# Attention values projected by channel and turned back, and slot inputs requested two slots ahead

## What is computed

```python
def attention(x, Wq, Wk, Wv, Wo):
    Q, K, V = x @ Wq, x @ Wk, x @ Wv
    logits = einsum('bqd,bkd->bqk', Q, K) * 128 ** -0.5
    attn = softmax(where(causal, -inf, logits))
    return einsum('bqk,bkd->bqd', attn, V) @ Wo

def ffn(x, ...):                          # cut to what matters
    xln = ln(x, ln1_w, ln1_b)
    x = x + sigmoid(xln @ Wr) * (xln @ Wv) @ Wo
    h = ln(x, ln2_w, ln2_b)
    winners = argmax(bids(h))             # one of 3 experts per row
    hr = square(relu(einsum('nc,ech->enh', h, K_rwkv)))      # two experts of 256 -> 1024 -> 256
    out_rwkv = einsum('enh,ehc->enc', hr, V_rwkv)
    out_trans = h @ W1 * sigmoid((xln @ Ws) @ W2) @ W3
    return x + chosen(out_rwkv, out_trans, winners) * scale

x = x + 0.5 * ffn(layernorm(x))
x = x + attention(layernorm(x))
x = x + 0.5 * ffn(layernorm(x))
```

## Time and profile before

| | us |
|---|---|
| median of 3 runs | 1089.14 (1087.94 to 1089.94) |
| the profiled execution | 1091.29 |
| span of its trace | 1089.5 |
| PE busy | 1000.6 (92%) |
| DVE, ACT, POOL busy | 691.2, 564.8, 496.5 |
| mean granted TensorE clock | 0.970 of full |

### The profile page before, as it was taken

How to read it: one execution, slowest core, us unless ns; L and a number is a source line. 1 busy time by engine, 2 the same in 40 slices (tenths; PEclk the granted TensorE clock), 3 DMA queues, 4 the chain that set the end, 5 groups by cost and what they waited for, 6 DMA issues and landing times.

```text
span 1089.5 us, 21438 instructions
## 1 busy us (share of the span) xinstructions
PE 1000.6 (92%) x7076; PEld 919.8 (84%) x7077; DVE 691.2 (63%) x1750; ACT 564.8 (52%) x1185; POOL 496.5 (46%) x541
## 2 busy tenths in 40 slices
PE   8999998959999999889988899899999699999997
PEld 7788886959999999778887788678888599999997
DVE  5688877836555554456765668578887764555553
ACT  5776655434454443245553555676664264444552
POOL 3254634456566556551221001135634576556665
PEclk8999998779999999999999999999999799999999
DMA  8621243122111111310222233402212222112211
GB/s 269 200 95 67 90 136 136 59 63 75 59 48 58 58 59 59 100 37 11 87 98 87 78 117 127 145 20 102 75 40 79 78 79 61 58 48 68 77 59 41
DMA packets 51845, 90.01 MB, mean 83 GB/s; under 512 B 5902, under 2 KB 44176, under 8 KB 50576
## 3 DMA queue, kind: packets, MB, share of 16 engines
q1 hardware_dynamic: 43120, 63.64, 18.7%
q0 software_dynamic: 8640, 25.24, 6.2%
HBM read 59.44 MB, written 47.85 MB: 98 GB/s over the span
## 4 chain that ended last, share of the span: by engine, by line
PE 66%; DVE 16%; DMA 6%; ACT 5%; issue 4%; POOL 3%; SPq 1%; DVEq 0%; POOLq 0%; ACTq 0%
PE banks4to L407 32%; PE bank L407 22%; PE banks4to L1694 3%; DMA slot_z<-routed_rows 2%; DVE out_rows L1053 2%; DVE pT_lo L1955 2%; PE bank L1227 2%; PE bank L503 1%; DVE gT_lo L955 1%; PE bank L1706 1%; DVE zT_lo L944 1%; DVE chunk_max L1945 1%; DMA attn_x<-x_after_ffn 1%; PE bank L371 1%; DMA routed_rows<-out_rows,row_index 1%
## 5 line engine op out<-in xcount | busy, mean ns | idle before, releaser
L1385 DVE TENSOR_TENSOR relu_squared<-relu 128x512 f32<-128x512 f32 x136 | 154.9, 1153 | 105.7 <-ACT relu L1336 55.3
L1451 POOL TENSOR_TENSOR hr_lo<-relu_squared,hr_hi 128x512 fp32r<-128x512 f32 x136 | 188.4, 1398 | 59.8 <-DVE relu_squared L1385 55.3
L1336 ACT ACTIVATE relu<-bank,slot_k_bias 128x256 f32<-128x256 f32 x204 | 84.8, 467 | 185.4 <-PE bank L407 168.0
L407 PE MATMUL banks4to<-v_hi,hr_hi 128*128 128x256 f32 x544 | 156.6, 288 | 3.7 <-DVE slot_out L1394 3.0
L407 PE MATMUL banks4to<-v_hi,hr_lo 128*128 128x256 f32 x544 | 153.3, 282 | 0.0
L407 PE MATMUL banks4to<-v_lo,hr_hi 128*128 128x256 f32 x544 | 153.3, 282 | 0.0
L407 PE MATMUL bank<-shT_hi,k_hi 128*128 128x256 f32 x408 | 116.9, 287 | 8.2 <-issue 5.4
L407 PE MATMUL bank<-shT_lo,k_hi 128*128 128x256 f32 x408 | 115.2, 282 | 0.0
L407 PE MATMUL bank<-shT_hi,k_lo 128*128 128x256 f32 x408 | 114.9, 282 | 0.0
L407 PEld LDWEIGHTS banks4to<-v_hi,hr_hi 128*128 128x128 f32 x544 | 103.5, 190 | 7.5 <-issue 7.0
L407 PEld LDWEIGHTS banks4to<-v_hi,hr_lo 128*128 128x128 f32 x544 | 103.5, 190 | 0.0
(11 more groups left out here) (279 smaller groups left out, 3031.7 us busy)
## 6 DMA issues: line engine op xcount, KB each, us to landing
routed_rows<-in_pad SPq DMA_DIRECT2D x34, 514.0 KB, 5.2
slot_row<-routed_rows SPq DMA_DIRECT2D x34, 258.0 KB
slot_z<-routed_rows SPq DMA_DIRECT2D x34, 256.0 KB
attn_x<-x_after_ffn SPq DMA_DIRECT2D x16, 256.0 KB, 2.9
attn_out<-x_after_ffn SPq DMA_DIRECT2D x16, 256.0 KB, 2.7
x_after_attention<-attn_out SPq DMA_DIRECT2D x16, 256.0 KB, 2.1
x_rows<-x_after_attention SPq DMA_DIRECT2D x8, 512.0 KB, 5.1
x_rows<-in_x SPq DMA_DIRECT2D x7, 512.0 KB, 4.0
```

The lines of the kernel that those rows point to most:

```text
L407: mm = pe.matmul(outv, w(pw), m(pm), start=(n_first and k == 0), stop=(n_last and k == 2))
L1336: last = act.activation(b.r[q % 2][:, (h % 2) * SLOT:(h % 2 + 1) * SLOT], b.bank(1 + q)[:, (h % 2) * SLOT:(h % 2 + 1) * SLOT], ACT.Relu, b ...
L1385: dve.tensor_tensor(b.sq[q % 2][:, :], b.r[q % 2][:, :], b.r[q % 2][:, :], ALU.mult).then_inc(f["sq"], 1)
L1451: pool.tensor_tensor(b.hr[p][1][:, 2 * q:2 * q + 2].rearrange("p h n -> p (h n)"), b.sq[q % 2][:, :], b.hr[p][0][:, 2 * q:2 * q + 2].rearr ...
```

## The change

Two edits that don't touch each other.

**Values.** `project_v` now holds the weights and streams the block's 256 rows, 2 x 3 = 6 matmuls of 256 columns. The result has channels on partitions. ACT copies it to a new tile `values_by_channel` (`v_turned`), PE turns its two halves back into columns 256 to 511 of the same bank (`turn_v`, 2 transposes), and only then come `v_hi` and `v_lo`. In the prologue the values of block k use bank k % 4 of banks 0 to 3, which takes V out of the ring there, and are turned after the next block's `project_qk`. In the steps they stay in the ring.

**Slots.** SP requests z two slots ahead: z of slots 0 to 3 before the wait for the late halves, then row(j), z(j+2).

In the diff the first piece is SP's, the pieces with `project_v` and `turn_v` are PE's, then one of ACT, and last two of DVE.

```diff
-    for j in range(2):
-        sp.dma_start(b.sz[j][:], rg[j][:, :, 0:C]).then_inc(f["s_in"][j], 16)
+    for j in range(4):
+        z_in(j, j % 2)
     sp.wait_ge(f["late"], 16 * GT * 2)
     for j in range(2):
-        sp.dma_start(b.srow[j][:, :, 0:ROW - C], rg[j][:, :, C:ROW]).then_inc(f["r_in"][j], 16)
-    with sp.Fori(0, (NSLOT - 3) // 2) as it:
+        row_in(j, j)
+    with sp.Fori(0, (NSLOT - 5) // 2) as it:
         for par in range(2):
-            slot_in(it * 2 + 2 + par, par)
-    slot_in(NSLOT - 1, 0)
+            row_in(it * 2 + 2 + par, par)
+            z_in(it * 2 + 4 + par, par)
...
     def project_v(k):
-        out = b.bank(k - QB + 4) if k in LATE_V else bank(("V", k))
+        out = b.bank(k % 4) if k < QB else bank(("V", k))
+        for c in range(CC):
+            mm = passes(pe, out[:, 0:SLOT], lambda p: b.Wvv[:, c, p * DK:(p + 1) * DK], lambda p: z_of(k)[p][:, c],
+                        c == 0, c == CC - 1)
+        mm.then_inc(a["V"], 1)
+
+    def turn_v(k):
+        pe.wait_ge(a["vt"], k + 1)
+        to = value_slot(k)
         for t in range(ST):
-            for c in range(CC):
-                mm = passes(pe, out[:, t * DK:(t + 1) * DK], lambda p: z_of(k)[p][:, c, t * P:(t + 1) * P],
-                            lambda p: b.Wvv[:, c, p * DK:(p + 1) * DK], c == 0, c == CC - 1)
-        mm.then_inc(a["V"], 1)
+            mm = pe.transpose(v_bank(b, k)[:, SLOT + t * DK:SLOT + (t + 1) * DK], b.vt[:, 2 * to + t], b.ident[:])
+        mm.then_inc(a["VN"], 1)
...
         project_qk(k)
+        if 0 <= k - 1 and k - 1 not in LATE_V:
+            turn_v(k - 1)
         if k not in LATE_V:
+            if k >= 4:
+                pe.wait_ge(a["vlo"], k - 3)
             project_v(k)
...
         if ks:
             project_v(ks[0])
         for k in ks[1:]:
             zT(k)
         weigh_some(s - 1, min(half + 2, n), n)
+        if ks:
+            turn_v(ks[0])
...
             if ks and i == min(1, late - 1):
-                v_hi(ks[0])
+                v_turned(ks[0])
...
+        for k in LATE_V if s == 0 else ks[:1]:
+            v_hi(k)
...
-        if s == 0:
-            for k in LATE_V:
-                v_lo(k)
...
+        for k in LATE_V if s == 0 else ks[:1]:
+            v_lo(k)
```

More of the change, by code:

```diff
@@ L214, in build_kernel @@
                       o_out=[sem(f"f{i}_slot_out{k}") for k in range(2)]) for i in range(2)]
-        names = ("stats", "z", "T", "zhi", "zlo", "QK", "V", "rstd", "zf", "qkhi", "qklo", "vhi", "vlo", "S", "nb", "exp", "PT", "pthi",
+        names = ("stats", "z", "T", "zhi", "zlo", "QK", "V", "rstd", "zf", "qkhi", "qklo", "vhi", "vlo", "S", "nb", "exp", "PT", "pthi", "vt", "VN",
                  "ptlo", "PV", "ohi", "olo", "Y", "y", "link", "plink")
@@ L1554, in score_banks @@
         order.append(("QK", k))
-        if k < QB - 2:
-            order.append(("V", k))
         if k + 2 < QB:
@@ L1578, with v_bank @@
 LATE_V = (QB - 2, QB - 1)
+def v_bank(b, k):
+    return b.bank(k % 4 if k < QB else 4 + BANK_AT[("V", k)] % 4)
 def attention_sync(sp, b, a, cleared, f, xg, pad, routed):
@@ L1776, in attention_tensor @@
                 scores(s, 1, c)
+        if s == 0:
+            for k in LATE_V:
+                turn_v(k)
         weigh_some(s - 1, half, min(half + 2, n))
@@ L1812, in qk_hi, with v_turned @@
         act.copy(b.kq[0][:, q], bank(("QK", k)).rearrange("p (m n) -> p m n", m=2)).then_inc(a["qkhi"], 1)
-    def v_hi(k):
+    def v_turned(k):
         to = value_slot(k)
@@ L1818, in v_hi @@
             act.wait_ge(a["PV"], pairs_before(k - QB))
-        out = b.bank(k - QB + 4) if k in LATE_V else bank(("V", k))
-        act.copy(b.v[0][:, 2 * to:2 * to + 2], out[:, 0:SLOT].rearrange("p (t n) -> p t n", t=ST)
+        act.copy(b.vt[:, 2 * to:2 * to + 2], v_bank(b, k)[:, 0:SLOT].rearrange("p (t n) -> p t n", t=ST)).then_inc(a["vt"], 1)
+    def v_hi(k):
+        to = value_slot(k)
+        act.wait_ge(a["VN"], k + 1)
+        act.copy(b.v[0][:, 2 * to:2 * to + 2], v_bank(b, k)[:, SLOT:2 * SLOT].rearrange("p (t n) -> p t n", t=ST)
                  ).then_inc(a["vhi"], 1)
@@ L1852, in attention_scalar @@
         qk_hi(k)
+        if 0 <= k - 1 and k - 1 not in LATE_V:
+            v_hi(k - 1)
         if k not in LATE_V:
-            v_hi(k)
+            v_turned(k)
         if k + 2 < QB:
@@ L1933, in v_lo @@
         dve.wait_ge(a["vhi"], k + 1)
-        out = b.bank(k - QB + 4) if k in LATE_V else bank(("V", k))
-        dve.tensor_tensor(b.v[1][:, 2 * to:2 * to + 2], out[:, 0:SLOT].rearrange("p (t n) -> p t n", t=ST),
+        dve.tensor_tensor(b.v[1][:, 2 * to:2 * to + 2], v_bank(b, k)[:, SLOT:2 * SLOT].rearrange("p (t n) -> p t n", t=ST),
                           b.v[0][:, 2 * to:2 * to + 2].bitcast(F32), ALU.subtract).then_inc(a["vlo"], 1)
@@ L1981, in attention_vector @@
         qk_lo(k)
-        if k not in LATE_V:
-            v_lo(k)
+        if 0 <= k - 1 and k - 1 not in LATE_V:
+            v_lo(k - 1)
         if k + 2 < QB:
@@ L2015, in attention_vector @@
             pair(s - 1, j)
-        if ks:
-            v_lo(ks[0])
         for k in ks[1:]:
```

9 lines of the change are left out of this document (8 added, 1 removed).

## The result

Over four runs each, after takes 1070.2 us (1068.16 to 1072.87), before 1088.54 (1087.36 to 1089.94): ratio 0.9832, 95% interval 0.9807 to 0.9858. The profiled execution of after took 1069.64 us.

A forecast was written before the change was run, and what follows sets the result against it. PE, busy 92% of the span, was taken to bound the kernel, with gains in its waits. First slots 9.0, other waits 2.7 and attention 0 sum to 11.7 us off 1089.14, giving 1077.4; range 1073.5 to 1081.5.

The forecast's parts named there:

- First slots, 9.0: First layer's slots: K(2) starts 10.6 us earlier, less 1.6 for the slow clock; net 9.0, bounds 8.0 and 10.6.
- The chain through POOL: First layer: POOL's late halves, then hrlo(1), sq(1) and slo(2) set K(2)'s start, at about 230.6 us.
- The other five waits go entirely ... 2.7 us; bounds 1.5 and 3.0: Remaining slots: PE's five listed `slot_z` waits besides slot 2's vanish, gaining 2.7 us.
- each restart also cost a slow first matmul: Slots: reason given for the upper bound of 3.0 us on the gain from the five small waits.
- Nothing replaces them: Slots: once the five small waits go, K(j) and V(j-1) wait for nothing else in these steps.
- The projection on PE: Values: a block takes 0.98 us instead of 1.34, 0.36 cheaper on PE alone, 5.8 us for 16 blocks.
- Prologue and step 0, 2.1: Attention's start: 0.7 us gained in the prologue through earlier statistics, about 1.4 in step 0 through earlier second maxima.
- Steps 1 to 4, -2.4: Attention: later `v_lo` delays DVE's queue and PE waits for `pT_lo`; each step loses 0.5 to 0.7 us, 2.4 in all.
- Steps 5 and 6, nothing: Attention: DVE waits 1.25 us for x from memory in the first, so the later `v_lo` fits in; no change.
- Attention in all, -0.1 taken as 0: Whole attention: 0.7 + 1.4 - 2.4 + 0.2 = -0.1 us, taken as 0; bounds +2.5 and -4.
- 1, 3 and 4: Turning costs more, 1082 us (chance 0.13); z(2) still late, 1086.5 (0.03); ACT's copy delays steps, slower than before, 1093.5 (0.03).
- Rival 2: More is gained: clock stays up in K(2), 10.6 instead of 9.0, and attention gains 1.5; 1074 us, chance 0.13.

The follow-up runs named there:

- stats_first: The changed kernel, but in attention's steps DVE does the row statistics of the block two further on before the values' low part; 1070.9 us, ratio 0.9838.
- halves_after: The changed kernel, but POOL subtracts slot 1's low part before sending the last rows' remaining halves in the first layer; 1073.05 us, ratio 0.9859.
- slots_only: The kernel before with SP's new order for the slots alone, attention as before; 1070.59 us, ratio 0.9838.
- values_only: The kernel before with the new projection and turning of the values alone, slots as before; 1086.74 us, ratio 0.9997.
- wait_K: The changed kernel with one wait added: PE turns slot j+1 only once K(j)'s last matmul is reported done; 1088.72 us, ratio 1.0004.

## Why the prediction was wrong, point by point

- **First slots, 9.0: right, in each part.** K(2) 10.54 us earlier (10.6), the clock's fall 1.58 (1.6; its size varies, 2.7 in stats_first). The chain through POOL was the right one, as halves_after shows. The wait was 3.49 where 3.3 was given.
- **"The other five waits go entirely ... 2.7 us; bounds 1.5 and 3.0": the step that failed.** It measured 9.5 to 10, and the 6.8 us missing even by the lower of these are the whole miss: 11.7 + 6.8 = 18.5, measured 18.3. The mechanism was right (z behind row's wait). The size was taken from the list of waits, which holds only those that show as idle time with a releaser. At the five turnings themselves the distance is 3.6 us over 0.12, not 2.7; others come up to 0.26 late without an entry, 1.2 in sum; and V comes up to 0.4 late behind a turning that is late or only just in time, 4.6 in sum, with 0.8 more inside V. The bound "each restart also cost a slow first matmul" asked for the right thing at five places instead of 30. What would have shown it was at hand: from K's last matmul to V's first it is 0.47 to 1.55 us in the slots of before behind slot 2, where one step of 0.12 and four transposes of 0.35 make 0.47.
- **"Nothing replaces them": right.** The distances of after are 0.12 and 0.35 in every slot.
- **The projection on PE: right.** In step 2 of after the six matmuls and the one behind them are

```profile
507.00 0.40 PE L408 MATMUL banks4to<-attn_zT_hi,wv_hilo 128*128 128x256 f32 x2
...
507.71 0.29 PE L408 MATMUL bank<-pT_hi,values_hi 128*128 128x256 f32 x1
```

0.71 us from start to start, as forecast, where twelve short ones take 1.34: the rule on short and long matmuls that the forecast weighed, which is one for isolated matmuls, does not hold for this stream. The two transposes take 0.28 more (508.63 to 508.91), where 0.27 was forecast. PE's 11.3 us less of busy time are not this edit's alone: slots_only, with the old projection and its 7076 matmuls, is busy 989.9 us, hardly more than after's 989.3, and values_only, with 7012, 995.2, 5.4 under before.

- **Prologue and step 0, 2.1: somewhat too high.** 1.4 between the two profiles; on the mean of all profiles 47.2 with the old and 45.6 with the new code, 1.6.
- **Steps 1 to 4, -2.4: right.** -2.15, and stats_first shows the cause that was given. **Steps 5 and 6, nothing: right in kind**; x from memory does set them: with x requested earlier they shrink, and with the 2.4 us won ahead of them alone (stats_first) the time does not fall.
- **Attention in all, -0.1 taken as 0: right.** values_only is 0.9997 of before.
- **Rivals.** 1, 3 and 4 did not occur. Rival 2, more is gained, had the sign but neither of its two reasons. The range held only bounds of named terms; a term sized at under a third of its cost had no place in it.
- **What would show it.** "The second layer's slots gaining more than their 1.3 us of the five small waits" was named as a sign of error, and is what happened: 4.5.

## What to carry to other kernels

A list of waits gives the waits long enough to be listed, not the cost of a late input. Where an input is requested so that it lands as it is needed, measure the distance between the last instruction before and the first ones behind it in every round of the loop, and compare with the shortest: the sum of the excess is the gain. And a load's slack is cheap to buy: about half a microsecond more was enough for the whole of it, while a wait added with everything ready cost 18 us over 30 rounds.

Where a stage is fed from memory in time with its own progress, work saved ahead of it can be waited for again. Look for that before trimming the chain, and move the request first.

## What was unexpected in the hardware's behaviour

- A wait that is met only by the end of PE's previous work costs 0.31 us at the waiting instruction (0.43 against 0.12) and up to 0.36 more at the next group behind it (0.71 against 0.35) inside a loop, but 0.03 to 0.17 where the same code stands outside it; 17 to 18 us over 30 slots with no data late (wait_K).
- A loop on PE that goes round six times per layer cost 10 us in the two layers: 9.1 in gaps ahead of K, all gone when it was written out, while branches on a register's value inside cost nothing that shows. The Trainium skill (Runtime: NRT & Kernel Launch, Instruction fetch mechanics) says that taken branches interrupt the fetching of code and that written-out loops are preferred for it; this agrees in sign, and that section has no number for it.
- Behind the idle stretch of 3.49 us the granted clock was 0.50 from 229 to 232. In halves_after, where PE does not stand there, it stayed up (K(2) took 5.64), and fell behind the 5.22 us wait at V(1) instead. Its windows:

```profile
225.00:228.00 3.00, 3.00 (x27) 3.00 (x26) 0.00 (x0) 1.01 (x3) 2.54 (x4) 1.00 0.00 0
...
237.00:240.00 3.00, 3.00 (x15) 3.00 (x15) 1.19 (x2) 2.25 (x6) 2.29 (x3) 0.50 0.65 183
```
